# Two cross-attention stages of a decoder: undivided exponentials, division after the value product, a deeper software pipeline

## The reference, cut to what is computed

```python
xn, kvn = layer_norm(x), layer_norm(ctx)        # first one only
q, k, v = heads(xn @ w_q), heads(kvn @ w_k), heads(kvn @ w_v)   # 16 heads of 16
attn = softmax(where(mask == 0, -1e9, q @ k.T / 4))             # mask: first one only
out  = (attn @ v) @ w_proj + b_proj
x    = layernorm(x + out)
# second one: the same without norms and mask, with biases bq, bk, bv, bo
```

## Time and profile before

| what | us |
|---|---|
| median of three executions | 5106.6 (5098.6 to 5106.6) |
| the profiled execution, its time | 5094.0 |
| the profiled execution, its span | 5092.2 |
| PE busy in the span | 3936.6 |
| DVE busy in the span | 3440.4 |
| ACT busy in the span | 2699.3 |
| POOL busy in the span | 2524.3 |

### The profile page before, as it was taken

The page is one execution under the profiler, slowest core; times in us unless marked ns, Lnnn a source line. Parts: engine busy times, 40 slices in busy tenths (PEclk is TensorE's granted clock), DMA queues, the critical chain, the costliest instruction groups (busy, mean ns, idle before and its releaser), DMA issues. The chain is left out here.

```text
span 5092.2 us, 75652 instructions
## 1 busy us (share of the span) xinstructions
PE 3936.6 (77%) x23066; PEld 2783.6 (55%) x23066; DVE 3440.4 (68%) x5947; ACT 2699.3 (53%) x4768; POOL 2524.3 (50%) x2530
## 2 busy tenths in 40 slices
PE   7886888876894258878888888888887898984665
PEld 4554555546543236666666666666665565652333
DVE  4444777762237757777777777777776666667888
ACT  2222555542323147777777777777775555543454
POOL 0001444430006648888888888888886333330011
PEclk9998999985875579999999999999998899997788
DMA  1111111113303311111111111111111001001111
GB/s 51 35 39 37 37 30 30 30 32 74 72 15 68 75 39 44 46 45 47 47 45 47 45 47 45 48 46 46 43 43 54 25 29 33 28 26 57 33 37 33
DMA packets 199788, 217.03 MB, mean 43 GB/s; under 512 B 27427, under 2 KB 164591, under 8 KB 199494
## 3 DMA queue, kind: packets, MB, share of 16 engines
q1 hardware_dynamic: 199494, 213.50, 14.5%
HBM read 162.03 MB, written 51.41 MB: 42 GB/s over the span
## 5 line engine op out<-in xcount | busy, mean ns | idle before, releaser
L2146 DVE TENSOR_TENSOR_SCAN ma_h<-ma_a,ma_pbu 128x512 f32<-128x512 f32 x1024 | 1211.9, 1208 | 426.2 <-PE ma_pbu L1767 348.8
L2036 POOL TENSOR_TENSOR ma_ch<-ma_h,ma_crep 128x512 f32<-128x512 f32 x1024 | 1321.1, 1306 | 270.0 <-DVE ma_h L2146 234.9
L1767 PE MATMUL ma_pbu<-ma_ident,ma_bu 128*128 128x128 f32 x4096 | 675.6, 291 | 151.0 <-DVE ma_h L2146 120.0
L1767 PEld LDWEIGHTS ma_pbu<-ma_ident,ma_bu 128*128 128x128 f32 x4096 | 507.4, 149 | 432.5 <-DVE ma_h L2146 281.9
L1776 PE MATMUL ma_py<-ma_ident,ma_ch 128*128 128x128 f32 x4096 | 656.7, 287 | 54.3 <-DVE ma_gT L2154 52.1
L1951 ACT ACTIVATE ma_a<-ma_dt,ma_A 128x510 f32<-128x510 f32 x1024 | 652.5, 715 | 5.7 <-DVE ma_h L2146 4.7
L752 POOL TENSOR_TENSOR xa_prob<-xa_e,xa_rec 128x616 f32<-128x616 f32 x256 | 312.8, 1222 | 594.5 <-DVE xa_rec L824 592.4
L1942 ACT ACTIVATE ma_bu<-ma_uT,ma_b_t 128x512 f32<-128x512 f32 x864 | 556.7, 717 | 67.0 <-PE ma_pbu L1767 65.1
L1776 PEld LDWEIGHTS ma_py<-ma_ident,ma_ch 128*128 128x128 f32 x4096 | 517.0, 149 | 58.8 <-issue 52.5
L683 ACT ACTIVATE xa_eT<-xa_pE 77x512 f32<-77x512 f32 x512 | 276.5, 586 | 351.5 <-PE xa_pE L565 351.5
L823 DVE TENSOR_REDUCE xa_esum<-xa_e 128x8 f32<-128x616 f32 x256 | 203.5, 795 | 235.4 <-ACT xa_e L678 235.4
(11 more groups left out here) (318 smaller groups left out, 7813.5 us busy)
## 6 DMA issues: line engine op xcount, KB each, us to landing
ma_crep<-ma_ct_dram SPq DMA_DIRECT2D x256, 256.0 KB, 3.3
ea_xg<-act SPq DMA_DIRECT2D x96, 256.0 KB, 4.9
xa_x<-act SPq DMA_DIRECT2D x64, 256.0 KB, 2.8
act<-xa_y SPq DMA_DIRECT2D x64, 256.0 KB, 2.2
la_x<-in_x SPq DMA_DIRECT2D x32, 256.0 KB, 3.4
act<-la_y SPq DMA_DIRECT2D x32, 256.0 KB
act<-scatter_yg SPq DMA_DIRECT2D x32, 256.0 KB, 4.1
ma_x<-act SPq DMA_DIRECT2D x16, 512.0 KB, 4.6
```

Source lines behind the costliest of these rows:

```text
L1767: last = pe.transpose(pbu[c % 2][:, t * P:(t + 1) * P], bu[:, s % 2, t, c * P:(c + 1) * P], ident[:, :])
L2036: pool.tensor_tensor(ch[:, s % 2, c], h[:, c], crep[:, s % 4, :], ALU.mult).then_inc(multiplied, 1)
L2146: dve.tensor_tensor_scan(out=h[:, c, :], data0=a[:, s % 2, c, :], data1=pbu[c % 2][:, :], initial=0.0, op0=ALU.mult, op1=ALU.add).then_inc ...
```

## The change

Only `cross_attention` is changed, for both stages.

- The transposes read `e` itself. `divide` on POOL and the tile `prob` are gone. `sums` now writes its reciprocal 16 times over, 128x128 (eight heads by 16 features), into one of four slots `rec`. `values` first transposes two such tiles into the free half of its bank (on PE), ACT copies them to `recT` (`copy_rec`, in the place of `copy_out`), and a new `divide` on DVE multiplies the product in PSUM by `recT` into `oT`.
- The engines' `batch` has five arguments instead of three. `scores` of a batch's units 0 and 1 run in the batch ahead of it, `turn_x` two batches ahead, `values(before,1)` and `project_out(before)` in the batch behind, `finish` two batches behind.
- k and v are made under one semaphore, in `pG[1]`; q in `pG[0]` with `project_out`. Context and mask have four slots. SP loads x once `residual` has read it, ahead of the store.
- The bias is folded: at the stage's start bv is multiplied by wo and added to bo, and `add_bias` on POOL adds that to x once a batch. The bias matmuls and their `split_in_three` are gone.

```diff
             def sums(j, b, u):
 
-                dve.wait_ge(e_ready, unit_number(j, b, u) + 1)
+                m = unit_number(j, b, u)
+                dve.wait_ge(e_ready, m + 1)
                 link(dve.tensor_reduce(esum[:, u % 2, :], e[:, u % 2].rearrange("p (h s) -> p h s", h=HC), AX.X, ALU.add))
-                dve.reciprocal(rec[:, u % 2, :], esum[:, u % 2, :]).then_inc(rec_ready, 1)
-
-            def batch(this, nxt, before):
+                if not (type(m) is int and m < 4):
+                    dve.wait_ge(oT_made, 2 * number(j, b) + (u // T - 1))
+                dve.reciprocal(rec[:, u], esum[:, u % 2, :].unsqueeze(2).broadcast_to([P, HC, DH])).then_inc(rec_ready, 1)
+
+            def divide(j, b, c):
+
+                dve.wait_ge(oT_made, 2 * number(j, b) + (c + 1))
+                dve.wait_ge(rec_copied, 2 * number(j, b) + (c + 1))
+                dve.tensor_tensor(oT[:, b % 2, c, :], pG[1 - c][:, 0:S], recT[:, c].rearrange("p t q -> p (t q)"),
+                                  ALU.mult).then_inc(oT_ready, 1)
+
+            def batch(this, nxt, after, before, two_before):
+                unit(*this, 2)
                 sums(*this, 1)
-                if nxt is not None and normed:
-                    norm_stats(*nxt)
+                if before is not None:
+                    divide(*before, 1)
+                if two_before is not None:
+                    finish(*two_before)
+                unit(*this, 3)
+                sums(*this, 2)
+                if after is not None and normed:
+                    norm_stats(*after)
+                if nxt is not None:
+                    unit(*nxt, 0)
+                divide(*this, 0)
+                sums(*this, 3)
+                if after is not None and normed:
+                    norm_apply(*after)
+                if nxt is not None:
+                    unit(*nxt, 1)
+                    sums(*nxt, 0)
                 if before is not None:
                     residual(*before)
...
-            def values(j, b, c):
-
+            def values(j, b, c, nxt):
+
+                pe.wait_ge(rec_ready, unit_number(j, b, T * c) + T)
+                if c == 0:
+                    pe.wait_ge(k_copied, number(*(nxt if nxt is not None else (j, b))) + 1)
+                    pe.wait_ge(v_copied, number(*(nxt if nxt is not None else (j, b))) + 1)
+                elif not (type(j) is int and j == 0 and b == 0):
+                    pe.wait_ge(res_added, number(j, b))
+                for t in range(T):
+                    pe.transpose(pG[1 - c][:, S + t * P:S + (t + 1) * P], rec[:, T * c + t, :, :].rearrange("p h e -> p (h e)"), ident[:, :])
                 pe.wait_ge(eT_copied, 2 * unit_number(j, b, T * c + T) + 2)
...
+            def add_bias(j, b):
+
+                pool.wait_ge(n_ready if normed else xT_made, number(j, b) + 1)
+                pool.tensor_tensor(x[:, b], x[:, b], bo[:, :].unsqueeze(1).broadcast_to([P, T, D]), ALU.add).then_inc(bias_added, 1)
+
+            def batch(this, nxt, after, before, two_before):
+                if nxt is not None:
+                    add_bias(*nxt)
+                    spread_k(*nxt)
+                if after is not None and normed:
+                    norm_scale(*after)
                 if before is not None:
                     rstd_of(*before)
```

More of the change, by code:

```diff
@@ L541, in project @@
[L541 to L544, removed]
             def scores(j, b, u):
                 p, c, t = b % 2, u // T, u % T
-                pe.wait_ge(low_ready, (4 * U) * j + (U * b + u + 1))
+                if u == 0:
+                    pe.wait_ge(kheads_ready, number(j, b) + 1)
+                    pe.wait_ge(q_copied, number(j, b) + 1)
@@ L616, in batch @@
-                turn(j, b, 2)
-                turn(j, b, 3)
-                if nxt is not None:
-                    first_scores(*nxt, 1)
-                    pe.wait_ge(v_copied, n + 1)
-                else:
-                    pe.wait_ge(v_copied, n)
-                values(j, b, 1)
+                    project_q(*nxt, before)
+                    scores(*nxt, 0)
+                turn(j, b, 2)
+                values(j, b, 0, nxt)
+                if before is not None:
+                    project_out(*before, 0, nxt)
@@ L625, in _ @@
+                if nxt is not None:
+                    scores(*nxt, 1)
+                if after is not None:
+                    turn_x(*after, this)
+                turn(j, b, 3)
+                if before is not None:
+                    project_out(*before, 1, nxt)
             pe.wait_ge(w_loaded, 16 * len(loads))
             pe.wait_ge(setup_done, 1)
-            front(0, 0)
-            project(0, 0)
-            first_scores(0, 0, 0)
-            first_scores(0, 0, 1)
+            if bv_d is not None:
+                for c in range(C):
+                    last = pe.transpose(pG[0][:, c * P:(c + 1) * P], bv[:, c * P:(c + 1) * P], ident[:, :])
+                last.then_inc(bv_turned, 1)
+                pe.wait_ge(bv_copied, 1)
+                for c in range(C):
+                    last = pe.matmul(pG[0][:, D:2 * D], bvT[:, c, :], wo[:, c, :], start=(c == 0), stop=(c == C - 1))
+                last.then_inc(bv_made, 1)
+                pe.wait_ge(bo_ready, 1)
@@ L886, in _ @@
             dve.sem_inc(low_ready, 2)
-            dve.sem_inc(res_added, 1)
+            if bv_d is not None:
+                dve.wait_ge(bv_made, 1)
+                dve.tensor_tensor(bo[:, :], bo[:, :], pG[0][:, D:2 * D], ALU.add).then_inc(bo_ready, 1)
             if normed:
-                norm_stats(0, 0)
-                norm_apply(0, 0)
+                for b in range(2):
+                    norm_stats(0, b)
+                    norm_apply(0, b)
             unit(0, 0, 0)
+            unit(0, 0, 1)
             sums(0, 0, 0)
-            unit(0, 0, 1)
             batches(dve, batch, link)
+            divide(*last_batch, 1)
+            finish(last_batch[0], last_batch[1] - 1)
             residual(*last_batch)
```

304 lines of the change are left out of this document (143 added, 161 removed).

## The result

The changed kernel takes 5131.56 us (median of 5 runs, 5124.01 to 5138.13) against 5102.87 us (5 runs, 5098.55 to 5106.6) for the kernel before: ratio 1.0056, 95% interval 1.0042 to 1.0071. It is slower by 28.7 us, where +43 was forecast.

The account below looks back on a forecast made before the run. PE, with the copies it waits for, bounds the kernel before; DVE would bound the changed one. xa1 +27, xa0 +18 and ends -2 make +43 us on the median 5106.6: 5150 us, range 5045 to 5225.

Parts of the forecast that it names:

- (a) The reciprocal: In `sums` on DVE: writing 128 elements a partition takes 953 ns, 0.75 us more, four times a batch: 3.0 us.
- the reciprocal doesn't grow: Rival: DVE's reciprocal stays as short, PE bounds the kernel, 16.7 us (xa1) and 18.7 (xa0), 4967 us; chance 0.04.
- (b): The new `divide` on DVE, 128x256 out of PSUM, twice a batch at 0.42 us: 0.84 us.
- (c): `finish` on DVE: 0.73 us with POOL idle, plus a 0.5 us stall (0 to 1.3) beside POOL's `spread_k`.
- The sum on DVE and its waits: DVE's work a batch, 17.1 us in xa1, 19.7 in xa0; with idle waits, full-clock periods of 19.1 and 19.9.
- The lower clock: PE pauses about 2.1 us before the scores, bringing a lower-clock stretch nearly every batch: 1.0 us (0 to 1.7).
- The ends: Start and end of both stages together: -6.4 + 4 = -2 us.
- the first rival: DVE holds, `finish` unhindered, lower clock beside the chain: 18.6 and 19.4 us a batch, 5050 us; chance 0.17.
- half the loss: Rival: only half of that loss, periods 19.4 (xa1) and 20.3 (xa0), about 0 change, 5105 us; chance 0.17.
- no loss: The same as the first rival: DVE bounds the batch and nothing else is lost, 5050 us; chance 0.17.
- Both get worse: Rival: two lower-clock stretches a batch, both instructions of `finish` stalled: 21.0 and 22.2 us, 5220 us; chance 0.13.
- Once a stage: Bias split gone, 5.1 us; xa1 gets 3.8 us folded-bias work; -6.4 together; last value product and division, +2 each.

Follow-up runs that it names:

- experiment 9: The changed kernel with the reciprocal cut back to 128x8 on VectorE and its 16-fold copies written by POOL: 4965.63 us, ratio 0.9730.
- experiments 7 and 10: 7: changed kernel, implied oT_made waits out, ScalarE's q copies ahead of slot 3's exponentials, 5006.14 us; 10: also reciprocal 128x8, widened on POOL, 4939.73 us.
- experiment 3: The changed kernel with 16 more VectorE instructions ahead of its loops, loop body unchanged: 5115.29 us, ratio 1.0025.
- The padded kernel of before: The kernel before with 22 more waits in each batch of VectorE's loops, all on an already full semaphore: 5124.73 us, ratio 1.0046.

## Why the prediction was right, point by point

- **(a) The reciprocal** was right to the nanosecond, 953 ns, and so was the direction: with it DVE is nearly the bound, with the narrow one (experiment 9) the kernel is 166 us faster than the changed one. Not all of that is the reciprocal: the clean jumps and the shorter pause are in it, and with both of these in place already it is worth 66 us (experiments 7 and 10). The rival "the reciprocal doesn't grow" put that kernel at 4967 us; 4965.6 was measured, with POOL's help, at 18.2 and 17.07 us a batch where 18.7 and 16.7 were worked out. So near it is by luck.
- **(b), (c)** held: the division is 0.36 to 0.42 us, and `finish` 1.16 us (1.09 from its start to the next instruction's) in xa1, 0.73 + 0.43, where 0.5 was put for `spread_k` beside it.
- **The sum on DVE and its waits** was 0.75 too high. A full-clock batch of xa1 is 18.35 us, not 19.1: DVE waits 1.2 for the division as worked out, 0.7 for the scores instead of 0.85, and its work, with handovers, is 16.45 instead of 17.1 (units take 1.48 to 1.53 us, not 1.61, up to the next instruction, and `finish` 1.09 to 1.11, not 1.23). In xa0 it is 19.47, not 19.9.
- **The lower clock** was mis-sized the other way, and is the term furthest off. The pause was right (2.13 for 2.1), also that every batch has such a stretch, but in xa1 it costs 1.96 us a batch, not 1.0, and more than the upper bound of 1.7: DVE's two waits grow by 0.7 and 1.1 us, so that the longer work (eight transposes 1.99 us instead of 1.10) is nearly all on the way that DVE waits for. In xa0 without the stalls the mean period of the 24 middle batches is 20.20 (experiment 3), 0.73 above full clock; 21.0 was forecast.
- **The ends** were sized at -2 us and are more. In xa1 the 24 middle batches average 20.49 us, which against 19.25 would be +40 us for 32, but the stage is only 21.6 us longer. The last two periods are 11.6 and 6.7 us, since the deeper pipeline empties there with no next batch to serve. Ahead of the batches the deeper pipeline costs: the first `residual` comes 63.4 us into xa1 instead of 49.6. With both, the ends give back some 18 us net in xa1; in xa0 19.4 us are saved in experiment 3, of which 32 x 0.24 = 8 in the batches and 11 at the ends.
- **What was to show it:** DVE is busy 15.98 us a batch in xa1 and 18.24 in xa0 (16.5 and 19 were named), the pause is there and ended by q's copy, `finish` is at 622 ns, and the clock over the long stretches is 0.91 in xa1 but 0.95 in xa0, where under 0.94 was named. By the prediction's own sign 0.95 is the first rival's, and xa0's batches of 19.46 us are near its 19.4.
- **Missing altogether** was the stall at VectorE's jumps (3.58 to 4.07 us of idle DVE and four instruction packets at each of five), some 20 us in xa0's batches, +16.4 by the stage lengths (696.3 - 679.9). The change made the body longer (267 instructions instead of 225) and its setup too, and so it begins at instruction 320 instead of 291; at 336 the same body doesn't stall. Nothing in the rows that the forecast rests on could show it.
- **Altogether:** xa0 was put at +18 and is 0, of which, with experiment 3 as the kernel without stalls, -19 are the change and +16 the stalls, and the rest is scatter; xa1 was put at +27 and is +21.6: the clock made it 31 us more, DVE's sum 24 us less and the ends some 17 us less; the other 5 us are about what every fourth period (20.95) is longer. +43 against +28.7 is partly luck: errors of 10 to 30 us cancel, and 7 of the 28.7 us lie where nothing was changed.

Rivals: half the loss (5105) and no loss (5050) put the lower clock at 0 to 0.5 us a batch; it is 1.96 in xa1. "Both get worse" (5220) needed 21.0 and 22.2 us. No run shows a reciprocal dearer than forecast, to which 0.03 was given; it is 953 ns. None came as a whole. The sum of "both get worse" is 110 by its own periods (32 x 3.51 - 2), not 113, which changes nothing here. The 3.8 us of new work for the folded bias, a term of "Once a stage", was measured by no run by itself.

## What to carry to other kernels

A copy that a stalled engine waits for goes ahead of one that has slack, even if it comes to the queue later: here two lines in ScalarE's order were worth 85 us, some 73 of them in xa1 and most of these through TensorE's clock (1.96 of 2.56 us in the batch shown), and nothing in xa0, where TensorE has another pause. An edit that looks cheap by its instruction count, such as a broadcast in a reciprocal, is to be priced by the elements that it writes (here 203 ns for 8 a partition, 953 for 128), and the same copies may be cheap on an idle engine, here POOL (403 ns each). When every n-th turn of a loop is long and n is its unrolling, look at the instruction queue's packets at the jump, and shift the loop by a few instructions before explaining it otherwise.

## What the runs showed of the hardware that I had not expected

- The place of a loop body decides whether a jump back stalls: 16 instructions ahead of the loop took five stalls away, 128 brought them back. One of them holds VectorE for 3.6 to 4.1 us and lengthens the batch by 4 to 8 us.
- The gain from removing the stalls was two thirds of their sum (20 of some 30 us from the first `residual` to the last).
- In xa1 a pause of 1.15 us on TensorE in each batch went with a granted clock of 1.00, one of 2.13 us with 0.91. Yet the full-clock batch of the changed kernel shown above has a pause of 1.9 us too and runs at 1.00, so the pause of a single batch doesn't tell its clock.
- The padded kernel of before loses 15.8 us in xa1. There TensorE's longest pause is 1.4 to 1.6 us in most batches instead of 0.9 to 1.1, and the clock over 4050 to 4500 us 0.92 instead of 0.95; by what way the waits on VectorE do that is not settled, nor why it loses 14.1 us in Mamba. The Mamba stage took 2151.1 to 2169.6 us in all profiles here, up to 5.4 us apart for the same kernel.
